# Expert stages: row loads and output stores interleaved on SyncE's queue, each load issued a body ahead

## The reference, cut to what matters

```
# first expert stage (layer 0): 8 experts, the best 2 per token, 256 hidden units
for e in range(n_experts):
    h = jax.nn.gelu(tokens @ w1[e].T, approximate=False)
    y = h @ w2[e].T
    out = out + gate[:, e:e + 1] * y

# second (layer 1): 8 experts, the best 2 per token, 512 hidden units, and a shared expert
up = jnp.einsum('th,ehi->tei', xf, up_w) + up_b
hact = jax.nn.gelu(up, approximate=False)
eo = jnp.einsum('tei,eih->teh', hact, down_w) + down_b
combined = jnp.einsum('teh,te->th', eo * 0.1, w)
shared = (jax.nn.gelu(xf @ sw_up + sb_up, approximate=False) @ sw_down + sb_down) * 0.1
```

## Time and profile before

| | |
|---|---|
| median of 3 runs | 1008.38 us (1006.87 to 1008.65) |
| the profiled execution | 1009.49 us, span 1007.5 us |
| PE busy | 814.3 us (81%) |
| DVE busy | 654.5 us (65%) |
| ACT busy | 479.2 us (48%) |
| POOL busy | 421.3 us (42%) |
| mean granted TensorE clock | 0.911 of full speed |
| layer 0, bodies | from about 158 to 272 us |
| layer 1, bodies | from about 792 to 949 us |

### The profile page before, as it was taken

One profiled execution on the slowest core, in us unless ns is written; L12 is line 12 of the kernel. 1 busy time (PEld: TensorE's weight loads), 2 busy tenths in 40 slices (PEclk: granted clock), 3 DMA queues, 4 the chain that ended last, 5 costly groups with the idle time before them and its releaser, 6 DMA issues. The chain is left out here.

```text
span 1007.5 us, 18830 instructions
## 1 busy us (share of the span) xinstructions
PE 814.3 (81%) x5585; PEld 608.3 (60%) x5585; DVE 654.5 (65%) x1525; ACT 479.2 (48%) x1001; POOL 421.3 (42%) x520
## 2 busy tenths in 40 slices
PE   2798716787626979999999999996458899999993
PEld 2566606787513545565656566545335799999862
DVE  4478644666756987777787777745731455568556
ACT  3375412222211556767676676773122365655520
POOL 3563667517337503233324332221067730174174
PEclk9899857999867999999999999995569899999997
DMA  5920014434314313213121312100012222233222
GB/s 161 363 68 1 32 47 136 120 104 135 95 68 135 102 30 97 72 54 101 39 94 35 105 63 64 32 1 0 0 43 74 71 87 72 78 107 96 80 58 73
DMA packets 82154, 80.44 MB, mean 80 GB/s; under 512 B 9856, under 2 KB 61758, under 8 KB 82110
## 3 DMA queue, kind: packets, MB, share of 16 engines
q1 hardware_dynamic: 73122, 62.68, 20.4%
q0 software_dynamic: 8192, 16.79, 5.6%
q10 hardware_dynamic: 796, 0.42, 0.2%
HBM read 41.06 MB, written 38.80 MB: 79 GB/s over the span
## 5 line engine op out<-in xcount | busy, mean ns | idle before, releaser
L1595 ACT ACTIVATE Pb<-ps,low 128x512 f32<-128x512 f32 x320 | 216.6, 689 | 133.2 <-PE ps L1694 87.6
L902 POOL DMA_INDIRECT YG<-yslots,slot x128 | 133.3, 1042 | 158.3 <-DMA yslots<-yb 88.2
L1473 DVE TENSOR_REDUCE m<-ps 128x4 f32<-128x1024 f32 x128 | 156.3, 1222 | 54.7 <-PE ps L1671 36.5
L1694 PE MATMUL ps<-Q,KZ 128*128 128x128 f32 (+3 forms) x512 | 172.2, 398 | 4.8 <-ACT Pb L1595 3.9
L390 POOL DMA_INDIRECT xslots<-XN,slot x128 | 125.4, 980 | 72.2 <-issue 37.6
L1397 POOL TENSOR_SCALAR_AFFINE_SELECT Pb<-Pb 128x512 f32<-128x512 f32 (+1 forms) x84 | 67.8, 807 | 190.6 <-ACT Pb L1595 190.0
L1239 PE MATMUL ps<-xT,wst 128*128 128x128 f32 x960 | 140.2, 285 | 5.9 <-DVE wst L1109 3.3
L1694 PEld LDWEIGHTS ps<-Q,KZ 128*128 128x128 f32 x512 | 93.0, 192 | 81.8 <-ACT Pb L1595 56.1
L1251 PE MATMUL ps<-wst,hb 128*128 128x128 f32 x960 | 137.1, 281 | 0.0
L1239 PEld LDWEIGHTS ps<-xT,wst 128*128 128x128 f32 x960 | 126.4, 201 | 7.3 <-DVE wst L1109 4.0
L1068 ACT ACTIVATE hb<-ps,upb 128x128 f32<-128x128 f32 x320 | 91.5, 369 | 76.9 <-PE ps L1239 76.9
(11 more groups left out here) (256 smaller groups left out, 1248.5 us busy)
## 6 DMA issues: line engine op xcount, KB each, us to landing
xt<-xslots SPq DMA_DIRECT2D x40, 256.0 KB
yslots<-yb SPq DMA_DIRECT2D x40, 256.0 KB, 2.4
terms<-high SPq DMA_DIRECT2D x32, 256.0 KB, 2.2
Q<-terms SPq DMA_DIRECT2D x128, 48.0 KB
KZ<-terms SPq DMA_DIRECT2D x128, 48.0 KB
xslots<-YG SPq DMA_DIRECT2D x2, 2560.0 KB, 11.7
terms<-low SPq DMA_DIRECT2D x16, 256.0 KB, 2.3
X<-in_L_attn_x_dram SPq DMA_DIRECT2D x4, 512.0 KB, 5.9
```

The costliest lines, as they stand in the source:

```text
L902: pool.indirect_dma_start(out=s.YG[:, TB * w + j, k, :], out_offset=None, in_=s.yslots[group][:, :], in_offset=bass.IndirectOffsetOnAxis(a ...
L1473: w = dve.tensor_reduce(top[:, :, (TB + 1, 3, TB, None, 1)[u]], ps.rearrange("p (t g k) -> p g t k", t=2, g=HG), AX.XY, ALU.max)
L1595: act.activation(Pb[:, NCH * (gg % 2) + c, :], bank(4 + c % 2), ACT.Exp, bias=s.low[:, :], scale=DH ** -0.5)\
L1694: w = pe.matmul(ps[:, col:col + T - kt * P], KZ[:, HG * gg + g, kt * P:kt * P + P], Q2[gg % 2][:, kt * P:T], start=True, stop=not masked)
```

## The change

In both expert stages SP's list is written in another order. Loads and stores alternate half by half; a store of body n - 1 stands where the store of body n stood, so that the load of body n + 1 is ahead of it. The wait for `scattered[1]` stands ahead of the first load of group 1, as before, but this load is now ahead of the stores of body 3 and not of body 4. No transfer is added or taken away, and the semaphore counts that each load and store waits for are the same.

```
-            def loads(g, n):
-                i = n + BODY0[g]
+            def load(g, n, r):
+                wait_apart(sp, x_turned, 2 * (n + BODY0[g]) + (r + 1))
+                sp.dma_start(xt[r][:, :, :], xrows[g][:, bass.ds(BT * n + TB * r, TB), :]).then_inc(x_load[r], 16)
+            def store(g, n, r):
+                wait_apart(sp, yb_ready, 2 * (n + BODY0[g]) + (r + 3))
+                sp.dma_start(yrows[g][:, bass.ds(BT * n + TB * r, TB), :], yb[r][:, :, :]).then_inc(stored[r], 16)
+            def rows_in(g):
+                sp.wait_ge(scattered[g], 16 * 2 * TB * GROUPS[g] * (layer + 1))
+            rows_in(0)
+            for r in two:
+                load(0, 0, r)
+            for g in range(NG):
                 for r in two:
-                    wait_apart(sp, x_turned, 2 * i + (r + 1))
-                    sp.dma_start(xt[r][:, :, :], xrows[g][:, bass.ds(BT * n + TB * r, TB), :]).then_inc(x_load[r], 16)
-            def stores(g, n):
-                i = n + BODY0[g]
+                    load(g, 1, r)
+                    if g > 0:
+                        store(g - 1, GB[g - 1] - 1, r)
+                with sp.Fori(1, GB[g] - 1) as n:
+                    for r in two:
+                        load(g, n + 1, r)
+                        store(g, n - 1, r)
+                if g + 1 < NG:
+                    rows_in(g + 1)
                 for r in two:
-                    wait_apart(sp, yb_ready, 2 * i + (r + 3))
-                    sp.dma_start(yrows[g][:, bass.ds(BT * n + TB * r, TB), :], yb[r][:, :, :]).then_inc(stored[r], 16)
-            for g in range(NG):
-                sp.wait_ge(scattered[g], 16 * 2 * TB * GROUPS[g] * (layer + 1))
-                loads(g, 0)
-                if g > 0:
-                    stores(g - 1, GB[g - 1] - 1)
-                with sp.Fori(0, GB[g] - 1) as n:
-                    loads(g, n + 1)
-                    stores(g, n)
-            stores(NG - 1, GB[NG - 1] - 1)
+                    if g + 1 < NG:
+                        load(g + 1, 0, r)
+                    store(g, GB[g] - 2, r)
+            for r in two:
+                store(NG - 1, GB[NG - 1] - 1, r)
```

## The result

The changed kernel takes 994.56 us (median of 4 executions, 989.27 to 994.72) against 1008.51: ratio 0.985, 95% interval 0.981 to 0.989. It is faster by 14 us, where 21.6 were forecast, and 994.56 lies above the range. The profiled execution took 994.72 us, span 992.9, against 1007.5: 14.6 us less.

The account below looks back on a forecast made before the run. PE was taken as the bound in layer 0's bodies 1 to 6 once rows are there, DVE in bodies 7 and 8. Terms -16.4 - 4.8 + 0.7 - 1.1 = -21.6 us gave 987 us, range 983.5 to 992.5.

Parts of the forecast that it names:

- Loads behind stores: Layer 0, bodies 1 to 6: loads go out a body ahead, so all six PE waits for `xt` go, -16.4 us.
- The clock in layer 0: Layer 0's expert stage: three clock dips behind PE's waits go, 1.6 us each, -4.8 us.
- The wait for group 1: Layer 0: SP stands at `scattered[1]` about 8 us, so body 5's rows come late, +0.7 us.
- rival B: Layer 0: POOL's 17 remaining scatters each take their worst time, body 5's rows 4.8 us later: 991.5 us; chance 0.07.
- Gathers: Layer 0, combine after body 6: first gather at 207.5, gathers ready 1.5 us before the combine at 220.6, cost 0.
- Bodies 7 and 8: Layer 0: DVE is the bound there and its 10.9 us cycle stays, so 0 us.
- Everything behind a stage starts at its barrier and moves with it.: All behind the expert stages, attention included: moves ahead with the stage's gain, no further term.
- Rival A: Expert stage: the clock dips stay or come elsewhere, price 4.8 us less what DVE's cycle absorbs, 990 to 992; chance 0.13.
- Layer 1: Layer 1's six bodies: small waits of 0.5 us and PE's pipeline restarts go, -1.1 us.
- Sum: Whole kernel: -16.4 - 4.8 + 0.7 - 1.1 = -21.6 us, forecast 987 us.

Follow-up runs that it names:

- `pairs`: The changed kernel, but SP issues both loads of a body and then both stores of the body two earlier, not interleaved: 990.05 us.
- `w_after`: The changed kernel plus 54 matmuls on PE at attention's head whose results nothing uses: 985.53 us, ratio 0.977.
- `delay2`: The changed kernel plus two DVE copies into a spare tile ahead of attention's first clearing: 990.14 us.
- `again`: The changed kernel run once more, unchanged, for its spread: 993.75 us.

## Why the prediction was wrong, point by point

*Loads behind stores.* Right. The six waits of 16.4 us are gone; the one that stands there now is another, for group 1's rows. A body was forecast at 8.2 us and measured 8.02. The 8.24 that I had taken contained the restart of PE after a wait. Five of the six restarts are gone (one wait is left), some 1 us more gained than forecast.

*The clock in layer 0.* Right: no dip in bodies 1 to 6. The stretch 162 to 172 us that I gave as a row at 1.00 has a mean of 0.98 in the trace; from 163 us on it is 1.00.

*The wait for group 1.* Right in mechanism, mis-sized: 1.55 us, not 0.7, since PE came there at 196.3 and not 196.9, and the load went out at 194.89 and not 194.65. From issue to use it took 3.0 us, forecast 2.9. The last scatter went out at 192.53, before at 192.42, so rival B did not come. The longer wait and the restarts cancel in the first combine, 220.62 for 220.6: that this number came out to the tenth is partly luck.

*Gathers.* Right: 207.60 for 207.5, and no combine waited for them.

*Bodies 7 and 8: "0, since the DVE cycle of 10.9 us stays".* Mis-sized. In bodies 7, 8 and 9 PE now stands for weights for 2.33, 2.12 and 2.47 us, and behind the first and third of these waits the clock falls. The first dip (227 to 231) isn't absorbed by the slack, and the cycle is 12.04 us; the next, without a dip, has 11.04. In `pairs` it is the other way round: 11.04 without a dip in body 7 (clock 1.00), 12.04 with one in body 8 (0.59 from 237 to 241). So a dip cost such a cycle 1.0 us. At the third combine the changed kernel is 19.1 us ahead, not 20.5; at attention 19.0. The cost is 1.5 us in all.

*"Everything behind a stage starts at its barrier and moves with it."* This is the step that failed. Attention moved forward by 19.0 us but didn't keep its length: 419.1 us for 413.6, so 5.4 us of the forecast gain were given back where I had put nothing. Its head is a stretch in which PE waits for DVE, then for DMA, and the clock granted over its 100 us was 0.81 and not 0.91. I had seen that the clock falls behind waits, and counted it only where the change was. Rival A (dips stay or come elsewhere, 990 to 992) is the nearest, with dips in bodies 7 to 9 as it says, but it stops at the end of the stage and at 4.8 us.

*Layer 1.* Right: from attention's end to the end of the span 317.2 us, before 318.3, 1.1 less.

*Sum.* -20.5 at the first combine, +1.5 to attention's start, +5.4 in attention, -1.1 in layer 1: -14.6, but for rounding. Against the forecast of -21.6 that is 1.5 us missing in bodies 7 to 9 and 5.4 in attention. What is shown by the runs is that attention's length goes with the clock of its head, and that matmuls put there take 3.5 us off the kernel before and 4 to 8 us off the changed one (by the ratios to the kernel before; no run of the changed kernel without them was made on the chip of `w_after`). What makes the clock of the head higher in one execution than in the next is open.

## What to carry to other kernels

In a queue that is worked in order, look at what stands ahead of a load and not at the load. One that waits for the end of a body makes every load behind it late, and moving it one body ahead took away the whole wait (2.3 to 3.8 us a body here) where the engine that needs the rows had no slack. Where a stage starts with short bursts of matmuls between waits, its length need not stay the same: a gain in the stage ahead can be given back there, so compare landmarks stage by stage, and take the clock of each head from the windows. Filling such waits with matmuls whose results nobody reads gained 3.5 us here before the change and 4 to 8 after it.

## What the runs showed of the hardware that I had not expected

A kernel can become faster by doing more: two more copies on DVE ahead of attention took 3.6 us off the median on one chip. (On another the changed kernel itself has 990.87, so the size is uncertain; ten of twelve executions under 992 against four of sixteen is the firmer sign.) The first cast there took 2.84 us beside a POOL memset of 1.81, and 1.21 us with two copies ahead of it, when that memset was over. From the start of the copies to the end of the cast it is then 3.59 us, so the 2.46 us of the two copies delayed what follows by only 0.75. In `delay2`'s trace:

```profile
254.45 2.46 DVE L1451 COPY pad<-zero 128x512 f32<-128x512 f32 x2 [4.72 <-PEq L985]
256.83 1.21 DVE L1452 CAST Q<-zero 128x2048 fp32r<-128x2048 f32 x1
```

In the changed kernel the clock fell behind waits of PE of 2.33 us (body 7) and 2.47 us (body 9) and not behind one of 2.12 us (body 8), but in `again` it fell behind 2.12 us in body 7 (0.61 from 226 to 230 us). In the kernel before it fell behind 2.76, 2.25 and 3.83 us, and in body 9 behind only 1.85 (0.50 from 269 to 271), but not behind 2.60, 2.58 and 2.34. The length of the wait alone does not tell.
